# Splitting the second pair's weights on GpSimd: copy and subtraction of a piece in one step instead of two

## The reference

```python
h = jnp.maximum(_layernorm(x, axis=-1), 0.0)
x = x + _L0_gnn_ref(h, Wq, bq, Wk, bk, Wv, bv, Wf, bf, adj)   # attention, 6 heads of 64
h = jnp.maximum(_layernorm(x, axis=-1), 0.0)
x = x + _L1_gnn_ref(h, adj, W, b, w_src, w_dst, H_w, H_b)     # graph attention, 12 heads of 32
# the same two once more, with the weights of L2 and L3
```

## Time and profile before

| | |
|---|---|
| median of 3 runs | 2045.95 us (2044.44 to 2047.39) |
| the profiled execution | 2046.12 us |
| its span | 2044.0 us |
| TensorE busy | 1971.7 us, 96% |
| ScalarE busy | 1910.9 us, 93% |
| VectorE busy | 1866.8 us, 91% |
| GpSimd busy | 1627.2 us, 80% |
| piece loads by SyncE (`stage<-w_vf`), issue to landing | 4.2 us at the median |

### The profile page before, as it was taken

The page is one execution under the profiler, slowest core; times in us unless marked ns, Lnnn a source line. Parts: engine busy times, 40 slices in busy tenths (PEclk is TensorE's granted clock), DMA queues, the critical chain, the costliest instruction groups (busy, mean ns, idle before and its releaser), DMA issues.

```text
span 2044.0 us, 58357 instructions
## 1 busy us (share of the span) xinstructions
PE 1971.7 (96%) x19596; PEld 1860.7 (91%) x19596; DVE 1866.8 (91%) x4249; ACT 1910.9 (93%) x6674; POOL 1627.2 (80%) x2859
## 2 busy tenths in 40 slices
PE   5999999999999999999999999999999999999973
PEld 4999999999999999999999999999999999999962
DVE  4699999999999999999999999999999999999884
ACT  3699999999999999999999999999999999999984
POOL 3578888888888888888888887888888888888773
PEclk9999999999999999999999999999999999999995
DMA  5022233233232222223331222222222222222121
GB/s 167 13 57 72 65 81 79 71 88 91 65 77 55 53 60 50 54 60 94 102 105 49 57 57 52 53 57 54 59 51 54 58 49 56 58 49 49 41 46 44
DMA packets 309330, 130.62 MB, mean 64 GB/s; under 512 B 229547, under 2 KB 308782, under 8 KB 309038
## 3 DMA queue, kind: packets, MB, share of 16 engines
q1 hardware_dynamic: 309038, 126.90, 24.2%
HBM read 69.42 MB, written 57.41 MB: 62 GB/s over the span
## 4 chain that ended last, share of the span: by engine, by line
PE 86%; DVE 5%; POOL 5%; issue 2%; ACT 1%; DMA 1%; SPq 0%; POOLq 0%; DVEq 0%
PE psum L766 36%; PE psum L776 18%; PE psum L840 5%; PE psum L851 4%; PE psum L817 4%; PE psum L862 4%; PE psum L758 4%; PE psum L823 3%; PE psum L828 3%; PE psum L804 3%; PE psum L872 2%; DVE LG L661 1%; DVE neg_max L665 1%; PE psum L810 1%; POOL prod L416 1%
## 5 line engine op out<-in xcount | busy, mean ns | idle before, releaser
L511 ACT ACTIVATE LG<-LG,neg_max 128x128 f32<-128x128 f32 x1536 | 595.8, 399 | 14.5 <-DVE neg_max L665 11.4
L511 ACT ACTIVATION_READ_ACCUMULATOR LG<-LG,neg_max 128x1 f32 x1536 | 305.0, 199 | 0.0
L505 ACT ACTIVATE LA<-LA,neg_max 128x128 f32<-128x128 f32 x768 | 296.6, 391 | 2.9 <-DVE neg_max L636 2.9
L661 DVE COPY_PREDICATED_SCALAR LG<-no_edge,no_edge_score 128x1536 f32 x127 | 252.5, 1988 | 6.2 <-ACT LG L578 2.4
L416 POOL TENSOR_TENSOR prod<-th,vec 128x384 f32<-128x384 f32 x256 | 255.5, 1021 | 2.2 <-ACT th L568 2.2
L665 DVE TENSOR_REDUCE neg_max<-LG 128x12 f32<-128x1536 f32 x127 | 222.7, 1753 | 13.9 <-DVE LG L661 0.5
L578 ACT ACTIVATE LG<-psum 128x1536 f32<-128x1536 f32 x127 | 185.3, 1459 | 48.1 <-PE psum L872 48.0
L636 DVE CUSTOM_DVE_ANT_0 LA<-psum,neg_bias 128x128 f32<-128x128 f32 x768 | 172.5, 288 | 57.3 <-PE psum L840 55.7
L776 PE MATMUL psum<-hT_hi,qk_hi 128*128 128x256 f32 x1152 | 212.2, 293 | 4.3 <-DVE hT_lo L692 4.3
L776 PE MATMUL psum<-hT_hi,qk_lo 128*128 128x256 f32 x1152 | 201.7, 283 | 0.0
L766 PE MATMUL psum<-hg_hi,gT_hi 128*128 128x384 f32 x768 | 190.8, 357 | 10.7 <-DVE gT_lo L684 10.7
(11 more groups left out here) (124 smaller groups left out, 6220.6 us busy)
## 6 DMA issues: line engine op xcount, KB each, us to landing
context<-gcT SPq DMA_DIRECT2D x512, 48.0 KB, 2.1
back<-context SPq DMA_DIRECT2D x128, 192.0 KB, 2.4
xin<-x SPq DMA_DIRECT2D x64, 192.0 KB, 2.5
x_mid<-x SPq DMA_DIRECT2D x64, 192.0 KB, 1.9
xin<-x_mid SPq DMA_DIRECT2D x64, 192.0 KB, 2.5
out<-x SPq DMA_DIRECT2D x64, 192.0 KB, 1.9
ahead<-stage SPq DMA_DIRECT2D x16, 288.0 KB, 4.0
stage<-w_qk SPq DMA_DIRECT2D x12, 192.0 KB, 3.6
```

Source lines behind the costliest of these rows:

```text
L505: last = act.activation(head, head, ACT.Exp, scale=-1.0, bias=neg_max[:, 0, h:h + 1], accum_out=rsum[:, h:h + 1])
L511: last = act.activation(head, head, ACT.Exp, bias=neg_max[:, 1, a:a + 1], accum_out=den[:, a:a + 1])
L661: dve.copy_predicated(LG_heads, no_edge[:, (k - 7) % 2, :].unsqueeze(1).broadcast_to([128, GH, N]), no_edge_score[:].unsqueeze(2).broadcas ...
```

## The change

`SPREAD` is 1, and `split_ahead` does both operations of a piece in one step: the copy, a wait for that copy, and the subtraction. The function's body loses its two branches. With `SPREAD = 1`, piece j is loaded in step 8 + j, split in step 9 + j and stored in step 11 + j. The splits are in steps 9 to 22 instead of 10 to 37, the load stands one step ahead of the split instead of two, and `divmod(k - AHEAD_STEP, SPREAD)` in `straight` gives a load and a store in each of these steps.

```diff
-SPREAD = 2
+SPREAD = 1
...
             def split_ahead(k):
 
-                j, part = divmod(k - AHEAD_STEP - SPREAD, SPREAD)
-                if 0 <= j < len(PIECES) and part < 2:
+                j = k - AHEAD_STEP - 1
+                if 0 <= j < len(PIECES):
                     m = len(PIECES) + j
                     n = PIECES[j][3]
                     src = stage[:, m % STAGES, :, 0:n]
                     hi = stage[:, (m + 4) % STAGES, :, 0:n]
-                    if part == 0:
-                        pool.wait_ge(w_in[m % STAGES], 16 * (m // STAGES + 1))
-                        if j >= 4:
-                            pool.wait_ge(s[f"ahead_out{j % 2}"], 32 * (j // 2 - 1))
-                        else:
-                            pool.wait_ge(s["w_split"], len(PIECES))
-                        pool.tensor_copy(hi.bitcast(F32R), src).then_inc(s["ahead_hi"], 1)
+                    pool.wait_ge(w_in[m % STAGES], 16 * (m // STAGES + 1))
+                    if j >= 4:
+                        pool.wait_ge(s[f"ahead_out{j % 2}"], 32 * (j // 2 - 1))
                     else:
-                        pool.wait_ge(s["ahead_hi"], j + 1)
-                        pool.tensor_tensor(src.bitcast(F32R), src, hi, ALU.subtract).then_inc(s["ahead_lo"], 1)
+                        pool.wait_ge(s["w_split"], len(PIECES))
+                    pool.tensor_copy(hi.bitcast(F32R), src).then_inc(s["ahead_hi"], 1)
+                    pool.wait_ge(s["ahead_hi"], j + 1)
+                    pool.tensor_tensor(src.bitcast(F32R), src, hi, ALU.subtract).then_inc(s["ahead_lo"], 1)
```

## The result

The changed kernel takes 2051.62 us (median of 10 runs, 2050.16 to 2052.97), the kernel before 2045.85 us beside it (10 runs): ratio 1.003, 95% interval 1.0021 to 1.004. It is slower, by 5.8 us; the forecast was 2051.3 us.

What follows compares the result with a forecast made beforehand. TensorE, with 86% of the chain, was taken to set the pace. The 14 split steps cost 8.1 us, less today's 2.8, net +5.3 on 2045.95: 2051.3 us, range 2047.2 to 2057.6.

Steps and rivals of the forecast that it cites:

- early step: Split step with GpSimd in its usual place: y passes between copy and subtraction; 15.05 us large, 14.90 small.
- Rival 1: At the split, GpSimd's subtraction always goes before y: 16.54 us per large step, net +11.0, 2057.0 us; chance 0.20.
- Rival 3: At the split, copy and subtraction never meet y, so today's 2.8 us go: 2043.1 us; chance 0.08.
- late steps: Split steps that GpSimd begins late: TensorE waits for L400, y for the subtraction; 17.08 us large, 16.10 small.
- large late step: Step begun with GpSimd 1.12 us late, large piece: L400 ends at 11.59, y at 17.16; 17.08 us.
- Rival 2: GpSimd's score parts slip past VectorE's L709 and L711, lateness mostly absorbed: net +2.2, 2048.2 us; chance 0.20.
- small late steps: Steps begun with GpSimd 0.71 us late, small piece: L400 ends at 11.18, y at 15.24; 16.10 us.
- large pair: Two split steps in turn with large pieces: 15.05 + 17.08 = 32.13 us, four times.
- last step: Final one of the 14 steps, giving back what TensorE had caught up: 14.75 us.
- sum of 14 steps: All split steps together: 221.25 us against 213.14 undisturbed, a cost of 8.1 us.

Runs made afterwards that it cites:

- e1: Changed kernel with copy and subtraction of each piece cut to one column per chunk, loads, stores and waits kept; 2043.0 us, ratio 0.999 to the kernel before.
- e8: Kernel before with a piece spread over three steps: copy, then the subtraction in two halves of the columns; 2042.41 us, ratio 0.9987.
- e3: Changed kernel with copy and subtraction of a piece together in one step, but only in every second step; 2051.52 us, ratio 1.0035 to the kernel before.
- e5: Changed kernel with the copy replaced by one memset and the subtraction by two, so the split is left out; 2044.27 us, ratio 1.0 to the kernel before.
- e6: Changed kernel with copy and subtraction moved from ahead of L406 to behind L408, that is behind y; 2064.51 us, ratio 1.0098 to the kernel before.
- e4: Changed kernel with GpSimd's five score parts moved ahead of hM; 2047.95 us, ratio 1.0015 to the kernel before.
- e7: Kernel before with GpSimd's five score parts moved ahead of hM; 2045.04 us, ratio 1.0002.
- e2: Changed kernel with only the copy cut to one column per chunk, the full subtraction kept in each step; 2050.11 us, ratio 1.0022 to the kernel before.

## Why the prediction was right, point by point

- That the place of the operations decides, and not their number: e1 has the split without its work, e8 has it spread over more steps, the changed kernel has it packed: 2043.0, 2042.4 and 2051.6 us.
- That y waits for the GpSimd operation under way, and passes the next one if it is there first: the early step's 0.41 us between copy and y; e3's small and large pieces, 0.10 and 0.05 us to either side. Rival 1 (GpSimd keeps its turn, 2057 us) falls with it: it would have needed 16.54 in each step with a large piece. Rival 3 (the pair never meets y) falls with the result: the copy starts 14.0 after the mark, as it did before. e5 adds that it is the reading of SBUF that excludes, a memset does not. The Trainium skill says the same (SBUF — State Buffer, Who interferes with whom): a VectorE instruction with two SBUF inputs contends with a GpSimd instruction that reads SBUF, not with one that only writes it. The traces agree: y takes 0.55 us beside e5's memset, 1.31 in e3 and 1.51 in the changed kernel beside a subtraction.
- That late steps are long by TensorE's waiting for L400 and by y's waiting for the subtraction: each gives about 1.0 us of a large late step. e6 has the first without the second and is 19.4 us slower than the kernel before; e4 cuts the first and keeps a wait of y for the copy, and is 3.0 slower, where the changed kernel is 5.8. For y's share alone the kernel before has the rows: with L400 on time, y ready at 14.45 instead of 14.73 and held for 0.86 us, its step is 15.79 long. Rival 2 (the score parts slip past) did not come: they took 0.41 and 0.55.
- That loads and stores are free: e1. No copy waited for its load: among GpSimd's waits in the changed kernel from 90 to 600 us none is for a transfer.
- Off were only sizes, most of all the term of the small late steps: 16.10 forecast, 16.37 measured. GpSimd is 0.87 us late at L406 there instead of the forecast's 0.71. L707 is at 9.92 after the mark at 148.10, L398, held by L709, takes 0.55 us, and L400 ends at 11.42 instead of the 11.18 of the sum:

```profile
158.02 0.54 DVE L707 SCALAR_TENSOR_TENSOR y<-y,ey 128x384 f32<-128x384 f32 x1
158.60 0.56 DVE L709 SCALAR_TENSOR_TENSOR y<-y,gate 128x384 f32<-128x384 f32 x1
158.71 0.55 POOL L398 TENSOR_TENSOR sd_rest<-sd_rest,sd 128x24 f32<-128x24 f32 x1
159.32 0.20 POOL L400 CAST sd<-sd_rest 128x24 bf16<-128x24 f32 x1
```

  The forecast gives only results for the small steps, so what it had left out of them can't be told. With 0.1 us in each large pair and 0.15 in the last step this makes the 1.0 us by which the sum of 14 steps was short.
- TensorE's waits for L690 (3.1 us of its weight loads) were not in the forecast. They stand in steps behind those in which the subtraction held y, and by them TensorE has caught up less than forecast: y is ready at 14.42 after the mark at 260.15 instead of 14.25. The pairs are no longer for it, since y then waits for the copy in any case. In the last step there is no copy, and it takes 14.90 us instead of 14.75.
- That the total came out nearer than the sum of steps is luck. The marks of the changed kernel stay 6.0 to 6.3 us behind those of the kernel before up to the 125th of the 128 (1992.94 against 1986.69 us). In the step that follows 0.3 us come back, and 0.1 behind the last mark, which is not explained.

## What to carry to other kernels

Ask of an added operation where in the engine's round it falls, which operation of the other engine would be held by it then, and how much each later result of that round has to spare; the engine's idle share (20% here) says nothing. Cut such work to pieces that end by the time the other engine needs its turn: here 0.8 us at a time cost nothing, 1.41 cost 0.4 in two steps, and a pair of 2.1 us cost 0.9 in each step. When results of a round have different slack, make the one with the least slack first; e4 got back about half of the loss by it, e7, where the loss had another cause, nothing.

## What the runs showed that I had not expected

Orders decided within 0.1 us change a step by 1 us: a large subtraction ready 0.06 us behind y (e2) lets GpSimd be late and gives steps of 14.73 + 16.75 us; in e3 a small one ready 0.10 us ahead of y gives 15.98 + 14.75. GpSimd late by 0.5 us at L406 (e5) delayed L400 by as much as 0.87 us late did in the changed kernel (it ended at 11.41 and 11.42 after the mark), since in both VectorE's L687 went ahead of L427; late by 0.10 it cost 0.09.
